# Hop-matrix building in a GNN kernel: 3, 2, 3, 2 sub-batches per turn in both passes, weighting on VectorE alone

## The chip, the cores and the metric

The kernel runs on one core of one Trainium2 chip. The metric is the device time of one execution in microseconds (us). Engines are named as the profile names them: PE is TensorE, PEld its weight loads, DVE is VectorE, ACT is ScalarE, POOL is GpSimd, SP is SyncE.

## The reference

Four graph layers run over the same 6,250 nodes (64 features) and 206,250 edges, which are sorted by destination. Each layer is `x = x + layer(relu(layernorm(x)))`:

```python
x = x + L0(h)   # h[src] @ W_msg + b, summed by dst; plus h @ W_self + b; rows divided by their norm
x = x + L1(h)   # h[src] @ W[type of the edge], summed by dst
x = x + L2(h)   # three hops of emb = segment_sum(w_e * emb[src], dst); mean of emb_0 .. emb_3
x = x + L3(h)   # an edge network's weight times h[src] @ W_src, summed by dst; plus h @ W_tgt
```

The three hops of L2 multiply by the same sparse matrix B (destination by source, with the edge weights as values).

## The kernel before

**Order of the work.** After a preparation of about 185 us, the kernel runs message pass 0 (layer L0), a projection that writes the relation table, message pass 1 (layer L1), the three hops (layer L2), and the edge pass (layer L3).

**A message pass.** The edges are cut into 1,664 steps (13 columns of 128) of 128 edges for one block of 128 nodes; 1,612 of them hold tiles of edges. Eight steps make a group (`G = 8`), four groups a turn (`R = 4`), so a pass has 208 groups in 52 turns (`ITER`). For each group:

- ACT copies eight index columns into `idx` (L739). The copy for group g + 3 waits for the products of group g.
- POOL starts eight indirect gathers of 128 rows (L540), which wait for that copy. Only 202 groups have gathers (`GQ`), 1,616 in a pass.
- DVE builds the one-hot tile `S` of the next group (L1312).
- PE multiplies `S` by the gathered rows (L977), into `ps[6]` and `ps[7]`.
- DVE adds the eight results into the accumulators (`accumulate`, L1326).

**Building B beside it.** B is needed only by the hops, and is built during the two message passes, as 62 chunks (`NCH`) of 16 sub-batches (`SUBS`), 992 in all. A sub-batch is `matrix_part`: DVE compares a column with an iota to make `ohp` in PSUM (L1366) and `Rc` (L1367), and multiplies `ohp` by the edge weights to make `Lw` (L1369). PE multiplies the two in 8 products (L959) and adds one to `bmm`, ACT copies the result to `stg` (L716) and adds one to `bev`, and SP writes each quarter of a chunk to `B_d` (L463). The buffers have two halves, so sub-batch u of DVE waits until the product of sub-batch u - 2 is done. Once per chunk the next chunk's records are loaded by SP (L447) and turned into columns by DVE, PE and ACT (L1331 to L1348, L944, L950, L707).

**How the sub-batches are spread.** `PER_TURN = (3, 2)`: every group of pass 0 builds three sub-batches, every group of pass 1 two, until the 62 chunks are done, which is after 46 of its 52 turns. Pass 0 builds 39 chunks (624 sub-batches), pass 1 23 (368). In pass 0 the second of the three sub-batches of a group is weighted by ACT (`by_scalar`, `weight_part`): DVE makes only `Rc` (L1363) and `ohp` (L1364) and ACT scales the eight slices one by one (L725). PE takes it by another semaphore, `lhs_a`.

**The loops.** `message_turns` unrolls whole bodies, because the half of a buffer and the place in a chunk must be constants: 8 turns in pass 0, 4 in pass 1 (`BODY`). In pass 0 turns 0 to 7 are written out, a loop runs over five bodies (turns 8 to 47), and turns 48 to 51 are written out; so the loop's branch is taken back four times.

Of the kernel before, what the change touches and what calls it, by code (L numbers as in the profile page):

```python
# [7 lines left out]
I32 = mybir.dt.int32  # L8
I16 = mybir.dt.int16
BF16 = mybir.dt.bfloat16  # L10
ALU = mybir.AluOpType
# [3 lines left out]
P = 128  # L15
# [6 lines left out]
def gnn_kernel(nc, x, src, dst, edge_attr, etype, eweight, msg_wt, msg_b, self_wt, self_b, lin, rel_w,  # L22
# [36 lines left out]
    SUBS = P // G  # L59
    PER_TURN = (3, 2)  # L60
    BODY = (8, 4)
    BUILT0 = ITER * R * PER_TURN[0] // SUBS
    FIRST = (0, BUILT0)
    CHUNKS = (BUILT0, NCH - BUILT0)
    BUILD_ITERS = tuple(k * SUBS // (R * t) for k, t in zip(CHUNKS, PER_TURN))
    assert all(i * R * t == k * SUBS and i <= ITER for i, k, t in zip(BUILD_ITERS, CHUNKS, PER_TURN)) and NCH <= KP
    assert all(b * R * t % (2 * SUBS) == 0 for b, t in zip(BODY, PER_TURN)) and min(BUILD_ITERS) > max(BODY)
    QS = SUBS // R
# [7 lines left out]
    PER_SLOT = [len(range(r, GQ, R)) for r in range(R)]  # L76
    assert NODE_BLOCKS - 1 <= (RS - 3) * G and GQ % (RS * R) >= R and GQ * G <= STEPS and (ITER - 3) * R + R - 1 < GQ - 3 + R

    with ExitStack() as ctx:
# [45 lines left out]
        def part(words):  # L125
# [39 lines left out]
        t0R = sb("t0R", [1, KP], I32)  # L165
        c128 = sb("c128", [P, NCH])
        ends = sb("ends", [P, 2])
        dcolAll = sb("dcolAll", [P, NCH])
        dvI = sb("dvI", [P, NCH], I32)
        dvH = sb("dvH", [P, NCH], I32)  # L170
        stepVi = sb("stepVi", [P, NCH], I32)
        stepV = sb("stepV", [P, NCH])
        start2 = sb("start2", [P, NC])
# [72 lines left out]
            mlp_Tc mlp_mm mlp_c web_in rec_out start_out start_in base_mm tcol_ok stair_f stair_T stair_e  # L246
            lhs_a types_in weights_in flat_ok flat_T flat_mv tiles_ok stair_done dve stair_d x_in ln_var ln_std ln_ok hs_ok hT_ps ht_ok proj_ps
            half_ps half_mv proj_mv nrm_in nrm_out idx_ok pc_ok rec2_out beg_oh beg_ps off_in off_ps tile_in tile_ps iota_ok
# [62 lines left out]
        def message_turns(n, eng, body):  # L311

            size, turn = BODY[n], PER_TURN[n]
            per_body = size * R * turn // SUBS

            def parts(b, k):
                at = [[(k * R + r) * turn + t for t in range(turn)] for r in range(R)]
                return [[(b * per_body + (FIRST[n] + o // SUBS), o % SUBS, (FIRST[n] + o // SUBS) % 2) for o in row] for row in at]

            def whole(b, count):  # L320
                for k in range(count):
                    body(b * size + k, parts(b, k))

            whole(0, size)
            with eng.Fori(1, BUILD_ITERS[n] // size) as b:
                whole(b, size)
            whole(BUILD_ITERS[n] // size, BUILD_ITERS[n] % size)
            if BUILD_ITERS[n] < ITER:
                none = [[] for r in range(R)]
                with eng.Fori(BUILD_ITERS[n], ITER - 3) as i:  # L330
                    body(i, none)
                for i in range(ITER - 3, ITER):
                    body(i, none)

        def next_chunk(row, pos):

            for c, at, h in row:
                if at == pos and not (isinstance(c, int) and c == NCH - 1):
                    return c + 1, 1 - h
            return None  # L340

        def by_scalar(n, t):

            return n == 0 and t == 1

        def weighted(n, g, t):

            if by_scalar(n, t):
                return s_["lhs_a"], g + 1
            if n == 0:  # L350
                return s_["lhs_ok"], g * 2 + (1 + (t > 1))
            return s_["lhs_ok"], g * PER_TURN[1] + (NG * 2 + t + 1)

# [153 lines left out]
        def _(pool):  # L507
# [9 lines left out]
            pool.iota(tile_i[:], [[P, NC]], base=0, channel_multiplier=1).then_inc(s_["pool_const"], 1)  # L517
            pool.iota(stepVi[:], [[P, NCH]], base=0, channel_multiplier=1).then_inc(s_["pool_const"], 1)

# [57 lines left out]
        def _(act):  # L577
# [139 lines left out]

            def weight_part(c, h, j):

                u = c * SUBS + j  # L720
                ohp = ps[2 + 3 * (j % 2)][:].rearrange("p (s k) -> p s k", s=G)
                act.wait_ge(s_["ohp_ok"], u + 1)
                for k in range(G):
                    at = 2 * P + j * G + k
                    ins = act.activation(Lw[:, j % 2, k, :], ohp[:, k, :], ACT.Copy, scale=cols[:, h, at:at + 1])  # L725
                ins.then_inc(s_["lhs_a"], 1)

            def message_pass(n, table):

                for r in range(R - 1):  # L730
                    act.wait_ge(s_["mm_ok"], n * NG + R)
                    act.copy(idx[:, r, :], table[:, r * G:(r + 1) * G]).then_inc(s_["idx_ok"], 1)

                def groups(i, parts):
                    for r in range(R):
                        if not (isinstance(i, int) and i * R + r + R - 1 >= GQ):
                            slot = (r + R - 1) % R
                            act.wait_ge(s_["mm_ok"], i * R + (n * NG + R + r + 1))
                            act.copy(idx[:, slot, :], table[:, bass.ds((i * R + (R - 1 + r)) * G, G)]).then_inc(s_["idx_ok"], 1)  # L739
                        for t, (c, pos, h) in enumerate(parts[r]):  # L740
                            if by_scalar(n, t + 1):
                                later = parts[r][t + 1]
                                weight_part(later[0], later[2], later[1])
                            matrix_part(c, pos)
                        ahead = next_chunk(parts[r], 9)
                        if ahead:
                            columns_of(*ahead)

                message_turns(n, act, groups)
# [98 lines left out]
        def _(pe):  # L848
# [103 lines left out]

            def matrix_part(n, g, t, c, j):

                pe.wait_ge(*weighted(n, g, t))
                wait(pe, s_["bev"], c * SUBS + (j - 1))
                for t in range(G):
                    a, i2 = t % 2, t // 2
                    ins = pe.matmul(ps[3 + j % 2][a * KP:(a + 1) * KP, i2 * KC:(i2 + 1) * KC], Lw[:, j % 2, t, :], Rc[:, j % 2, t, :],  # L959
                                    start=True, stop=True)  # L960
                ins.then_inc(s_["bmm"], 1)
# [3 lines left out]
            def segment(n):  # L965

                def groups(i, parts):
                    for r in range(R):
# [10 lines left out]
                        ins.then_inc(s_["mm_ok"], 1)  # L979
                        for t, (c, pos, h) in enumerate(parts[r]):  # L980
                            matrix_part(n, i * R + r, t, c, pos)
                        ahead = next_chunk(parts[r], 5)
# [134 lines left out]
        def _(dve):  # L1117
# [231 lines left out]

            def matrix_part(n, t, c, h, j):  # L1350
# [11 lines left out]
                if by_scalar(n, t):  # L1362
                    dve.tensor_tensor(Rc[:, j % 2, :, :], column(1, KC), iota_view(0, KC), ALU.is_equal)  # L1363
                    dve.tensor_tensor(ohp, column(0, KP), iota_view(0, KP), ALU.is_equal).then_inc(s_["ohp_ok"], 1)  # L1364
                    return
                dve.tensor_tensor(ohp, column(0, KP), iota_view(0, KP), ALU.is_equal).then_inc(s_["ohp_ok"], 1)  # L1366
                dve.tensor_tensor(Rc[:, j % 2, :, :], column(1, KC), iota_view(0, KC), ALU.is_equal)  # L1367
                dve.wait_ge(s_["ohp_ok"], u + 1)
                dve.tensor_tensor(Lw[:, j % 2, :, :], ohp, column(2, KP), ALU.mult).then_inc(s_["lhs_ok"], 1)  # L1369

            def message_pass(n, acc):
# [5 lines left out]
                def groups(i, parts):  # L1377
                    for r in range(R):
                        g = i * R + r
                        if not (isinstance(g, int) and g == NG - 1):  # L1380
                            one_hot(n, g + 1, (r + 1) % 2)
                        for t, (c, pos, h) in enumerate(parts[r]):
                            matrix_part(n, t, c, h, pos)
                        ahead = next_chunk(parts[r], 3)
# [40 lines left out]
            dve.sem_inc(s_["emb_ok"], 1)  # L1425
            chain(dve.tensor_scalar(dvI[:], dcolAll[:], float(PAD_DST), None, ALU.min))
            dve.tensor_scalar(dvH[:], dvI[:], 7, None, ALU.logical_shift_right)
# [129 lines left out]
```

## Time and profile before

| | |
|---|---|
| time, median of 3 runs | 8172.84 us (8172.44 to 8179.2) |
| profiled execution, its own time | 8187.84 us |
| span of the profiled execution | 8185.5 us |
| PE, DVE, ACT, POOL busy | 69%, 57%, 23%, 59% of the span |
| first gather of pass 0, first gather of pass 1 | 185.91 us, 2445.26 us |
| mean granted TensorE clock | 0.682 |

The span is the time from the first to the last instruction of one profiled execution, and it lies 2.3 us below that execution's own time. That execution was 15 us, or 0.18%, above the median. Busy shares are means over stages that are limited by different things, so they don't say what bounds a stage.

### The profile page before, as it was taken

The page shows a single profiled execution, that of the slowest core. Times are in us where ns is not written, and L with a number is a line of the kernel's source. Part 1 is how long each engine was busy: PE and PEld are TensorE (multiplying, and loading weights), DVE is VectorE, ACT ScalarE, POOL GpSimd, SP SyncE. Part 2 cuts the span into 40 slices and gives each one's busy share as a digit, 9 for nine tenths or more (in the row PEclk, how much of TensorE's full clock was granted, in tenths as well). Part 3 has the DMA queues.
Part 4 walks back from the last instruction along what each step waited for, and adds up shares of the span by engine and source line. Part 5 has one row for each costly group of instructions (what it writes and reads, how often), then busy time and mean ns, then how long its engine had stood idle before and what let it go on. Part 6 is the DMA issues. An engine that isn't in the chain of part 4 may idle for free.

```text
span 8185.5 us, 140527 instructions
## 1 busy us (share of the span) xinstructions
PE 5623.4 (69%) x42670; PEld 4173.2 (51%) x42671; DVE 4634.9 (57%) x10227; ACT 1864.4 (23%) x5982; POOL 4830.8 (59%) x5107
## 2 busy tenths in 40 slices
PE   3777666667755665566654777778768777877776
PEld 2666666666635555555554222222245555555555
DVE  5888888888856677777763000000045555555555
ACT  2333333333341111111110000000033333333333
POOL 1777777777707777777776111111137777777776
PEclk6666666666675656665665899999966666666666
DMA  6555555555644444444441999999933333333332
GB/s 192 90 92 92 92 89 92 88 93 88 92 163 69 71 69 71 73 72 69 71 73 39 400 426 405 426 406 426 426 101 81 83 81 82 82 81 83 81 82 68
DMA packets 795088, 1178.07 MB, mean 144 GB/s; under 512 B 617420, under 2 KB 645485, under 8 KB 766911
## 3 DMA queue, kind: packets, MB, share of 16 engines
q1 hardware_dynamic: 624379, 931.36, 37.7%
q0 software_dynamic: 164496, 230.86, 14.9%
q10 hardware_dynamic: 5684, 9.22, 0.4%
q8 instruction: 281, 4.60, 0.3%
q14 instruction: 248, 2.03, 0.1%
HBM read 919.30 MB, written 258.34 MB: 144 GB/s over the span
## 4 chain that ended last, share of the span: by engine, by line
POOL 31%; issue 19%; DMA 19%; PE 16%; DVE 12%; ACT 2%; DVEq 2%; SPq 0%; POOLq 0%; ACTq 0%
POOL arena L572 15%; POOL arena L540 15%; DMA arena<-B_d 13%; PE ps L1030 4%; PE ps L959 4%; PE ps L977 4%; DMA arena<-tab,idx 3%; DVE pair L1326 2%; DVE arena L1369 2%; DVE arena L1367 2%; DMA arena<-rec_d 2%; DVE ps L1366 2%; ACT arena L725 1%; DVEq L1318 1%; DVE arena L1363 1%
## 5 line engine op out<-in xcount | busy, mean ns | idle before, releaser
L540 POOL DMA_INDIRECT arena<-tab,idx x3232 | 3050.2, 944 | 1246.4 <-issue 1161.4
L572 POOL DMA_INDIRECT arena<-tab,idx x1664 | 1591.5, 956 | 647.1 <-issue 640.4
L977 PE MATMUL ps<-arena 128*128 x6656 | 1262.4, 369 | 897.4 <-DMA arena<-tab,idx 799.2
L959 PE MATMUL ps<-arena 128*64 128x98 f32 x15872 | 1322.3, 344 | 623.7 <-ACT arena L725 321.6
L977 PEld LDWEIGHTS ps<-arena 128*128 128x128 f32 x6656 | 1204.4, 280 | 969.1 <-issue 967.8
L959 PEld LDWEIGHTS ps<-arena 128*64 128x64 f32 x15872 | 1133.1, 203 | 754.9 <-issue 545.4
L1030 PE MATMUL ps<-arena,ev 128*64 128x512 f32 (+1 forms) x4836 | 1103.5, 602 | 363.3 <-DMA arena<-B_d 275.0
L1030 PEld LDWEIGHTS ps<-arena,ev 128*64 128x64 f32 x4836 | 391.4, 143 | 1075.1 <-issue 736.4
L563 POOL DMA_INDIRECT ev<-emb_d,dvI x186 | 175.1, 942 | 1268.2 <-PE ps L1030 1027.6
L1312 DVE TENSOR_TENSOR arena<-relT,ps 128x1024 f32<-128x1024 f32 x624 | 758.5, 1216 | 117.5 <-issue 114.7
L1441 DVE COPY pair<-ps 128x512 f32<-128x512 f32 x9 | 5.7, 684 | 1426.7 <-PE ps L1030 1426.7
L1367 DVE TENSOR_TENSOR arena<-arena,ps 128x784 f32<-128x784 f32 x784 | 754.2, 962 | 0.0
L1057 PE MATMUL ps<-ident,arena 128*64 128x128 f32 x3328 | 384.2, 406 | 451.3 <-DMA arena<-tab,idx 451.3
L716 ACT COPY arena<-ps 128x392 f32<-128x392 f32 x992 | 491.6, 496 | 811.8 <-PE ps L959 794.6
L1057 PEld LDWEIGHTS ps<-ident,arena 128*64 128x64 f32 x3328 | 302.5, 208 | 710.1 <-DMA arena<-tab,idx 708.6
L1366 DVE TENSOR_TENSOR ps<-arena,ps 128x512 f32<-128x512 f32 x784 | 540.9, 690 | 137.1 <-PE ps L959 134.8
L1504 DVE TENSOR_TENSOR pair<-pair,ps 64x128 f32 x1664 | 475.0, 285 | 209.4 <-PE ps L1092 119.7
L1326 DVE TENSOR_TENSOR pair<-pair,ps 128x64 f32 x2496 | 514.1, 219 | 112.2 <-issue 103.1
L1326 DVE TENSOR_TENSOR X<-X,ps 128x64 f32 x832 | 183.1, 220 | 643.3 <-PE ps L977 608.6
L1369 DVE TENSOR_TENSOR arena<-ps,arena 128x512 f32<-128x512 f32 x784 | 534.2, 681 | 0.0
L1476 DVE TENSOR_TENSOR arena<-ps,arena 128x512 f32<-128x512 f32 x208 | 143.7, 691 | 668.2 <-ACT arena L821 668.2
L814 ACT COPY arena<-arena 128x192 bf16 x1664 | 440.4, 347 | 126.8 <-issue 126.8
(244 smaller groups left out, 4982.4 us busy)
## 6 DMA issues: line engine op xcount, KB each, us to landing
arena<-B_d SPq DMA_DIRECT2D x186, 3136.0 KB, 24.8
B_d<-arena SPq DMA_DIRECT2D x248, 784.0 KB
arena<-tab,idx POOLq DMA_INDIRECT x4896
arena<-rel_d SPq DMA_DIRECT2D x208, 256.0 KB, 3.4
tab<-arena SPq DMA_DIRECT2D x26, 1024.0 KB, 3.9
arena<-rec_d SPq DMA_DIRECT2D x63, 257.5 KB
attr_s<-arena SPq DMA_DIRECT2D x13, 512.0 KB, 3.2
arena<-attr_s SPq DMA_DIRECT2D x208, 32.0 KB
```

Source lines behind the costliest of these rows:

```text
L540: pool.indirect_dma_start(ring[:, at:at + D], None, table, bass.IndirectOffsetOnAxis(ap=idx[:, k % R, u:u + 1], axis=0)).then_inc(gather_o ...
L572: pool.indirect_dma_start(gat[:, r, k * 2 * D:(k + 1) * 2 * D], None, tab3, bass.IndirectOffsetOnAxis(ap=idx[:, r, k:k + 1], axis=0)).then ...
L716: act.copy(stg[:, r % 2, j * w:(j + 1) * w], ps[3 + j % 2][:, 0:w]).then_inc(s_["bev"], 1)
L959: ins = pe.matmul(ps[3 + j % 2][a * KP:(a + 1) * KP, i2 * KC:(i2 + 1) * KC], Lw[:, j % 2, t, :], Rc[:, j % 2, t, :], start=True, stop=True)
L977: ins = pe.matmul(ps[6 + r % 2][:, k * D:(k + 1) * D], S[:, r % 2, k, :], ring[:, bass.ds(at[k], D)], start=True, stop=True)
L1030: ins = pe.matmul(ps[k][h * D:(h + 1) * D, 0:n], ev[:, u % EVS, :], Bb[:, u % BUFS, c0:c0 + n], start=c == 0, stop=c == NCH - 1)
L1057: pe.matmul(ps[h][t * D:(t + 1) * D, q * P:(q + 1) * P], gv[:, r, k, D:2 * D], ident[:], start=False, stop=True, skip_group_check=True)
L1312: dve.tensor_tensor(S[:, h, :, :], steps_of(relT, g), iota_view(n, P), ALU.is_equal).then_inc(s_["S_ok"], 1)
L1326: dve.tensor_tensor(a, a, ps[6 + r % 2][:, k * D:(k + 1) * D], ALU.add).then_inc(s_["acc_ok"], 1)
L1366: dve.tensor_tensor(ohp, column(0, KP), iota_view(0, KP), ALU.is_equal).then_inc(s_["ohp_ok"], 1)
L1367: dve.tensor_tensor(Rc[:, j % 2, :, :], column(1, KC), iota_view(0, KC), ALU.is_equal)
L1369: dve.tensor_tensor(Lw[:, j % 2, :, :], ohp, column(2, KP), ALU.mult).then_inc(s_["lhs_ok"], 1)
```

## The change

`PER_TURN` now gives the sub-batches of the four groups of a turn, 3, 2, 3 and 2, in both passes. A body is 16 turns in both passes: 160 sub-batches, 10 whole chunks. A pass is one body written out, a loop over two more (its branch is taken back once), and four turns written out (`TAIL`). In the four last turns pass 0 builds two sub-batches per group (two chunks more) and pass 1 none. Pass 0 so builds 32 chunks (512 sub-batches) and pass 1 30 (480). All weighting is done by DVE: `by_scalar`, `weighted`, `weight_part` and the semaphore `lhs_a` are gone. The records of one chunk past the last are now prepared too (63 in place of 62), and four small tiles are one column wider.

```diff
-    PER_TURN = (3, 2)
-    BODY = (8, 4)
-    BUILT0 = ITER * R * PER_TURN[0] // SUBS
+    PER_TURN = (3, 2, 3, 2)
+    BODY = 16
+    PER_BODY = BODY * sum(PER_TURN) // SUBS
+    BODIES = ITER // BODY
+    TAIL = ITER - BODIES * BODY
+    TAIL_TURN = 2
+    BUILT0 = BODIES * PER_BODY + TAIL * R * TAIL_TURN // SUBS
...
         def message_turns(n, eng, body):
...
-            whole(0, size)
-            with eng.Fori(1, BUILD_ITERS[n] // size) as b:
-                whole(b, size)
-            whole(BUILD_ITERS[n] // size, BUILD_ITERS[n] % size)
-            if BUILD_ITERS[n] < ITER:
-                none = [[] for r in range(R)]
-                with eng.Fori(BUILD_ITERS[n], ITER - 3) as i:
-                    body(i, none)
-                for i in range(ITER - 3, ITER):
-                    body(i, none)
+            def whole(b):
+                for k in range(BODY):
+                    at = [k * sum(PER_TURN) + sum(PER_TURN[:r]) for r in range(R)]
+                    body(b * BODY + k, [[place(b * PER_BODY, at[r] + t) for t in range(PER_TURN[r])] for r in range(R)])
+
+            whole(0)
+            with eng.Fori(1, BODIES) as b:
+                whole(b)
+            for k in range(TAIL):
+                row = TAIL_TURN if n == 0 else 0
+                body(BODIES * BODY + k, [[place(BODIES * PER_BODY, (k * R + r) * row + t) for t in range(row)] for r in range(R)])
...
-            def weight_part(c, h, j):
-
-                u = c * SUBS + j
-                ohp = ps[2 + 3 * (j % 2)][:].rearrange("p (s k) -> p s k", s=G)
-                act.wait_ge(s_["ohp_ok"], u + 1)
-                for k in range(G):
-                    at = 2 * P + j * G + k
-                    ins = act.activation(Lw[:, j % 2, k, :], ohp[:, k, :], ACT.Copy, scale=cols[:, h, at:at + 1])
-                ins.then_inc(s_["lhs_a"], 1)
...
-                pe.wait_ge(*weighted(n, g, t))
+                pe.wait_ge(s_["lhs_ok"], c * SUBS + (j + 1))
...
                 wait(dve, s_["bmm"], u - 1)
-                if by_scalar(n, t):
-                    dve.tensor_tensor(Rc[:, j % 2, :, :], column(1, KC), iota_view(0, KC), ALU.is_equal)
-                    dve.tensor_tensor(ohp, column(0, KP), iota_view(0, KP), ALU.is_equal).then_inc(s_["ohp_ok"], 1)
-                    return
                 dve.tensor_tensor(ohp, column(0, KP), iota_view(0, KP), ALU.is_equal).then_inc(s_["ohp_ok"], 1)
```

## Rows read from the trace of the kernel before

**Rows 1.** Busy time by stretch: both passes with tails, the projection, hops, edge pass

```profile
core 0: us, PE busy (x) PEld busy (x) DVE busy (x) ACT busy (x) POOL busy (x), PEclk, DMA share, GB/s
185.00:2245.00 2060.00, 1423.63 (x13150) 1283.41 (x13152) 1748.00 (x3621) 675.64 (x2437) 1524.23 (x1615) 0.64 0.57 90
2245.00:2326.00 81.00, 61.83 (x544) 56.20 (x542) 67.88 (x150) 26.11 (x90) 0.94 (x1) 0.58 0.41 65
...
2445.00:4462.00 2017.00, 1166.09 (x9324) 1083.16 (x9324) 1348.74 (x3039) 230.68 (x589) 1524.48 (x1616) 0.60 0.42 67
4462.00:4493.00 31.00, 24.15 (x112) 23.97 (x112) 15.97 (x62) 0.00 (x0) 0.57 (x1) 0.50 0.10 3
```

**Rows 2.** The gathers of pass 0: durations, first and last start, their engine's idle time

```profile
L540 POOL DMA_INDIRECT arena<-tab,idx x1616: 938/944/1032, 185.9 to 2245.3; - x180
...
  issue: 479.9, 1562
  ACT idx L739: 55.3, 53
```

**Rows 3.** The same for the gathers of pass 1

```profile
L540 POOL DMA_INDIRECT arena<-tab,idx x1616: 940/944/1068, 2445.3 to 4461.6; - x180
...
  issue: 681.5, 1584
  ACT idx L739: 9.8, 32
```

**Rows 4.** Timeline of POOL in pass 0: a gather that follows at once, the longest waits

```profile
1178.70 0.94 POOL L540 DMA_INDIRECT arena<-tab,idx  x1 [0.30 <-issue]
...
859.11 0.94 POOL L540 DMA_INDIRECT arena<-tab,idx  x1 [4.34 <-ACT idx L739]
1188.35 0.94 POOL L540 DMA_INDIRECT arena<-tab,idx  x1 [8.70 <-ACT idx L739]
1518.08 0.94 POOL L540 DMA_INDIRECT arena<-tab,idx  x1 [7.42 <-ACT idx L739]
1849.36 0.94 POOL L540 DMA_INDIRECT arena<-tab,idx  x1 [6.94 <-ACT idx L739]
```

**Rows 5.** Timeline of DVE and PE ahead of the wait at 1188 us

```profile
1177.00 1.22 DVE L1312 TENSOR_TENSOR arena<-relT,ps 128x1024 f32<-128x1024 f32 x1 [3.28 <-issue]
1179.03 0.68 PE L977 MATMUL ps<-arena 128*128 x2 [4.52 <-DVE arena L1312]
1183.95 3.25 PE L977 MATMUL ps<-arena 128*128 x14 [4.24 <-issue]
```

**Rows 6.** DVE by line, pass 0 with its tail: busy, mean ns, idle before

```profile
L1326 DVE TENSOR_TENSOR pair<-pair,ps 128x64 f32 x1664 | 331.3, 219 | 107.8 <-issue 103.1 <-DVE pair L1326 3.1
L1366 DVE TENSOR_TENSOR ps<-arena,ps 128x512 f32<-128x512 f32 x416 | 287.9, 692 | 137.1 <-PE ps L959 134.8 <-issue 1.8
```

**Rows 7.** Timeline of DVE in pass 1: one group with two sub-batches, next one's start

```profile
2987.49 1.22 DVE L1312 TENSOR_TENSOR arena<-relT,ps 128x1024 f32<-128x1024 f32 x1
2988.63 0.69 DVE L1366 TENSOR_TENSOR ps<-arena,ps 128x512 f32<-128x512 f32 x1
...
2990.71 0.69 DVE L1366 TENSOR_TENSOR ps<-arena,ps 128x512 f32<-128x512 f32 x1
...
2994.32 1.22 DVE L1312 TENSOR_TENSOR arena<-relT,ps 128x1024 f32<-128x1024 f32 x1
```

**Rows 8.** Timeline of pass 0's tail: a sub-batch for ACT, the last sums, the next step

```profile
2271.26 0.96 DVE L1363 TENSOR_TENSOR arena<-arena,ps 128x784 f32<-128x784 f32 x1
...
2272.86 1.74 ACT L725 ACTIVATE arena<-ps,arena 128x64 f32<-128x64 f32 x8 [5.76 <-DVE ps L1364]
...
2325.13 1.44 DVE L1326 TENSOR_TENSOR pair<-pair,ps 128x64 f32 x8
...
2326.61 0.96 DVE L1408 TENSOR_TENSOR pair<-pair 128x768 f32<-128x768 f32 x1
```

**Rows 9.** Timeline of pass 1's tail: last gather, products and sums after it

```profile
4461.63 0.94 POOL L540 DMA_INDIRECT arena<-tab,idx  x1 [0.30 <-issue]
4466.71 24.15 PE L977 MATMUL ps<-arena 128*128 x112 [8.80 <-DMA arena<-tab,idx]
4470.52 0.22 DVE L1326 TENSOR_TENSOR X<-X,ps 128x64 f32 x1 [9.55 <-PE ps L977]
```

**Rows 10.** What PE waited for in pass 1: us in total, times, longest

```profile
PE ps L977 <- DMA arena<-tab,idx: 772.5, 131, 20.8
```

**Rows 11.** Timeline of PE in pass 0's tail: a sub-batch, a group's products

```profile
2271.39 1.58 PE L959 MATMUL ps<-arena 128*64 128x98 f32 x16 [2.76 <-DVE arena L1369]
...
2277.46 3.68 PE L977 MATMUL ps<-arena 128*128 x16
```

**Rows 12.** ACT by line: copies of products, weighting

```profile
L716 ACT COPY arena<-ps 128x392 f32<-128x392 f32 x992 | 491.6, 496 | 811.8 <-PE ps L959 794.6 <-issue 16.7
...
L725 ACT ACTIVATE arena<-ps,arena 128x64 f32<-128x64 f32 x1664 | 362.7, 329 | 409.1 <-DVE ps L1364 398.8 <-issue 9.1
```

More of the change, by code:

```diff
@@ L59, in gnn_kernel @@
     SUBS = P // G
-    PER_TURN = (3, 2)
-    BODY = (8, 4)
-    BUILT0 = ITER * R * PER_TURN[0] // SUBS
+    PER_TURN = (3, 2, 3, 2)
[5 more added lines that the diff above has]
+    BUILT0 = BODIES * PER_BODY + TAIL * R * TAIL_TURN // SUBS
     FIRST = (0, BUILT0)
     CHUNKS = (BUILT0, NCH - BUILT0)
-    BUILD_ITERS = tuple(k * SUBS // (R * t) for k, t in zip(CHUNKS, PER_TURN))
-    assert all(i * R * t == k * SUBS and i <= ITER for i, k, t in zip(BUILD_ITERS, CHUNKS, PER_TURN)) and NCH <= KP
-    assert all(b * R * t % (2 * SUBS) == 0 for b, t in zip(BODY, PER_TURN)) and min(BUILD_ITERS) > max(BODY)
+    assert BODY * sum(PER_TURN) == PER_BODY * SUBS and PER_BODY % 2 == 0 and TAIL * R * TAIL_TURN % SUBS == 0
+    assert BUILT0 % 2 == 0 and CHUNKS[1] == BODIES * PER_BODY and BODIES > 2 and TAIL >= 3 and NCH < KP
     QS = SUBS // R
@@ L76, in gnn_kernel @@
     PER_SLOT = [len(range(r, GQ, R)) for r in range(R)]
-    assert NODE_BLOCKS - 1 <= (RS - 3) * G and GQ % (RS * R) >= R and GQ * G <= STEPS and (ITER - 3) * R + R - 1 < GQ - 3 + R
+    assert NODE_BLOCKS - 1 <= (RS - 3) * G and GQ % (RS * R) >= R and GQ * G <= STEPS
     with ExitStack() as ctx:
@@ L165, in gnn_kernel @@
         t0R = sb("t0R", [1, KP], I32)
-        c128 = sb("c128", [P, NCH])
+        c128 = sb("c128", [P, NCH + 1])
         ends = sb("ends", [P, 2])
-        dcolAll = sb("dcolAll", [P, NCH])
+        dcolAll = sb("dcolAll", [P, NCH + 1])
         dvI = sb("dvI", [P, NCH], I32)
         dvH = sb("dvH", [P, NCH], I32)
-        stepVi = sb("stepVi", [P, NCH], I32)
-        stepV = sb("stepV", [P, NCH])
+        stepVi = sb("stepVi", [P, NCH + 1], I32)
+        stepV = sb("stepV", [P, NCH + 1])
         start2 = sb("start2", [P, NC])
@@ L246, in gnn_kernel @@
             mlp_Tc mlp_mm mlp_c web_in rec_out start_out start_in base_mm tcol_ok stair_f stair_T stair_e
-            lhs_a types_in weights_in flat_ok flat_T flat_mv tiles_ok stair_done dve stair_d x_in ln_var ln_std ln_ok hs_ok hT_ps ht_ok proj_ps
+            types_in weights_in flat_ok flat_T flat_mv tiles_ok stair_done dve stair_d x_in ln_var ln_std ln_ok hs_ok hT_ps ht_ok proj_ps
             half_ps half_mv proj_mv nrm_in nrm_out idx_ok pc_ok rec2_out beg_oh beg_ps off_in off_ps tile_in tile_ps iota_ok
@@ L311, in message_turns, with place @@
         def message_turns(n, eng, body):
[L313 to L322, printed above, removed]
-            whole(0, size)
-            with eng.Fori(1, BUILD_ITERS[n] // size) as b:
-                whole(b, size)
-            whole(BUILD_ITERS[n] // size, BUILD_ITERS[n] % size)
-            if BUILD_ITERS[n] < ITER:
-                none = [[] for r in range(R)]
-                with eng.Fori(BUILD_ITERS[n], ITER - 3) as i:
-                    body(i, none)
-                for i in range(ITER - 3, ITER):
-                    body(i, none)
+            def place(c0, o):
+                return c0 + (FIRST[n] + o // SUBS), o % SUBS, (FIRST[n] + o // SUBS) % 2
+            def whole(b):
[8 more added lines that the diff above has]
+                body(BODIES * BODY + k, [[place(BODIES * PER_BODY, (k * R + r) * row + t) for t in range(row)] for r in range(R)])
         def next_chunk(row, pos):
             for c, at, h in row:
-                if at == pos and not (isinstance(c, int) and c == NCH - 1):
+                if at == pos:
                     return c + 1, 1 - h
             return None
-        def by_scalar(n, t):
-            return n == 0 and t == 1
-        def weighted(n, g, t):
-            if by_scalar(n, t):
[L349 to L352, printed above, removed]
         def column_turns(eng, body):
@@ L517, in _ @@
             pool.iota(tile_i[:], [[P, NC]], base=0, channel_multiplier=1).then_inc(s_["pool_const"], 1)
-            pool.iota(stepVi[:], [[P, NCH]], base=0, channel_multiplier=1).then_inc(s_["pool_const"], 1)
+            pool.iota(stepVi[:], [[P, NCH + 1]], base=0, channel_multiplier=1).then_inc(s_["pool_const"], 1)
             pool.wait_ge(s_["rec_out"], 16 * 7)
@@ L739, in groups @@
                             act.copy(idx[:, slot, :], table[:, bass.ds((i * R + (R - 1 + r)) * G, G)]).then_inc(s_["idx_ok"], 1)
[L740 to L743, printed above, removed]
+                        for c, pos, h in parts[r]:
                             matrix_part(c, pos)
@@ L951, in record_columns, with matrix_part @@
                 ins.then_inc(s_["recT"], 1)
-            def matrix_part(n, g, t, c, j):
-                pe.wait_ge(*weighted(n, g, t))
+            def matrix_part(c, j):
+                pe.wait_ge(s_["lhs_ok"], c * SUBS + (j + 1))
                 wait(pe, s_["bev"], c * SUBS + (j - 1))
@@ L979, in groups @@
                         ins.then_inc(s_["mm_ok"], 1)
-                        for t, (c, pos, h) in enumerate(parts[r]):
-                            matrix_part(n, i * R + r, t, c, pos)
+                        for c, pos, h in parts[r]:
+                            matrix_part(c, pos)
                         ahead = next_chunk(parts[r], 5)
@@ L1348, in record_weights, with matrix_part @@
                 dve.tensor_tensor(d2, d2, w, ALU.mult).then_inc(s_["row_d"], 1)
-            def matrix_part(n, t, c, h, j):
+            def matrix_part(c, h, j):
                 def column(f, w):
@@ L1361, in matrix_part @@
                 wait(dve, s_["bmm"], u - 1)
-                if by_scalar(n, t):
-                    dve.tensor_tensor(Rc[:, j % 2, :, :], column(1, KC), iota_view(0, KC), ALU.is_equal)
-                    dve.tensor_tensor(ohp, column(0, KP), iota_view(0, KP), ALU.is_equal).then_inc(s_["ohp_ok"], 1)
-                    return
                 dve.tensor_tensor(ohp, column(0, KP), iota_view(0, KP), ALU.is_equal).then_inc(s_["ohp_ok"], 1)
@@ L1381, in groups @@
                             one_hot(n, g + 1, (r + 1) % 2)
-                        for t, (c, pos, h) in enumerate(parts[r]):
-                            matrix_part(n, t, c, h, pos)
+                        for c, pos, h in parts[r]:
+                            matrix_part(c, h, pos)
                         ahead = next_chunk(parts[r], 3)
@@ L1425, in _ @@
             dve.sem_inc(s_["emb_ok"], 1)
-            chain(dve.tensor_scalar(dvI[:], dcolAll[:], float(PAD_DST), None, ALU.min))
+            chain(dve.tensor_scalar(dvI[:], dcolAll[:, 0:NCH], float(PAD_DST), None, ALU.min))
             dve.tensor_scalar(dvH[:], dvI[:], 7, None, ALU.logical_shift_right)
```

## The prediction, made before the changed kernel ran

> **What bounds the kernel now.** I first cut the span into stretches [rows 1]. The change touches only pass 0 with its tail (185 to 2326 us) and pass 1 with its tail (2445 to 4493 us); the projection between them, the hops and the edge pass keep their instructions. No engine is full in either pass, so the busy shares do not name the bound. In pass 0 DVE is nearest to it (1748 of 2060 us), in pass 1 POOL is (1524 of 2017 us).
>
> Next I read the gathers. In both passes POOL issues 1616 of them, 944 ns each. In pass 1 the first starts at 2445.3 and the last at 4461.6: 2016.3 us, or 1.248 us from one to the next. That is 0.944 us of work and 0.30 us of issue, and almost nothing of it is waiting: the index copies cost 9.8 us in 32 waits [rows 3]. PE on the other hand waits 772.5 us for gathered rows [rows 10]. So pass 1 runs at POOL's pitch, 8 x 1.248 = 9.98 us per group, and everything else has room.
>
> In pass 0 the same 1616 gathers take 2245.3 - 185.9 = 2059.4 us, 43.1 us more [rows 2]. A gather that does not wait follows at the same pitch (0.94 + 0.30 us, [rows 4]), so the excess is waiting, and the trace has it: 55.3 us on the index copies [rows 2], less some us that are the normal gap of those gathers. The longest waits, 4.34, 8.70, 7.42 and 6.94 us, lie about 330 us apart, which is eight turns of some 41 us, the length of a loop body [rows 4]. Just ahead of such a wait DVE stands 3.28 us and PE 4.52 and again 4.24 us inside a group of products, with no work to wait for in the second case [rows 5]. I read this as the loop's branch being taken back. The index copy waits for PE's products, and POOL for the copy.
>
> But a hiccup of 9 us every 330 us costs time only where there is no reserve. The copy is made three groups ahead, and in pass 1 the branch back shows nowhere in POOL's waits. In pass 0 the reserve is used up by DVE. Its ledger over pass 0 and the tail: busy 1748.0 + 67.9 = 1815.9 us [rows 1], waiting 134.8 us for the product of two sub-batches ago, and 103.1 us of issue ahead of the sums [rows 6], together 2053.8 of 2141 us; the rest is in small waits around the records and the branches. DVE is the paced engine of pass 0, at 2053.8 / 208 = 9.87 us per group before those small waits, against POOL's 9.98 us. There is no slack to repay a hiccup.
>
> **The cost of a sub-batch.** On DVE a sub-batch starts 2990.71 - 2988.63 = 2.08 us after the one before [rows 7]. One that ACT weights omits L1369 and costs DVE about 1.48 us (L1363 starts at 2271.26, its second instruction ends before ACT's start at 2272.86, [rows 8]). ACT then takes 1.74 us for it, later than DVE would have been by about a microsecond, and DVE's third sub-batch waits for its predecessors' products: the 134.8 us.
>
> **Pass 0.** DVE's sub-batch work was 416 x 2.08 + 208 x 1.48 = 1173 us and becomes 512 x 2.08 = 1065 us: 108 us less. The waits on PE stay in one group of two at most: with three sub-batches by DVE, PE needs 3.68 + 1.58 us for the group's products and its first sub-batch [rows 11], and DVE comes to the third after 1.14 + 2 x 2.08 = 5.3 us, a draw. I take 30 us of the 134.8 as left; the ends are 0 and 134.8. The ledger becomes 2053.8 - 108 - 105 = 1841 us; with the 87 us of small waits left as they are, 1928 us, 9.27 us per group, and 9.77 if all of the 134.8 us stay. One more set of records in pass 1 doesn't change this. Both lie under 9.98 us, so DVE gives the bound to POOL and keeps a reserve. A group with three sub-batches takes 1.14 + 3 x 2.08 + 1.5 = 8.9 us, one with two 6.83 us (2994.32 - 2987.49, [rows 7]); even the long one is shorter than POOL's group, so the alternation alone builds up no delay. The branch is taken back once, not four times, and its 9 us are repaid within some ten groups. Gathers of pass 0: 2059.4 -> 2016.3 us, **-43.1 us**. Upper bound of what stays: one wait of 9 us.
>
> **Its tail.** From the last gather of pass 0 to the first step behind it 2326.6 - 2245.3 = 81.3 us pass [rows 2, 8], because the groups 202 to 207 have no gathers but full building, and because PE is behind. Pass 1 shows what a punctual PE does: its products start 5.1 us and its sums 8.9 us after the last gather's start [rows 9]. The sums take 1.5 us, and six groups follow with two sub-batches each: 6 x 6.83 = 41 us, and I add 3.6 us for the next records' instructions and gaps. 8.9 + 1.5 + 41 + 3.6 = 55.0 us, **-26.3 us**. Bounds: 51.4 us with no gaps, and 60 us with 8 us per group.
>
> **Pass 1.** It gains 112 sub-batches, 112 x 2.08 = 233 us of DVE work, on 1348.7 + 16.0 us busy [rows 1]: 1598 us of 2048, under 8 us per group. PE gets 112 x 1.58 = 177 us more on 1190 us [rows 1, 11], ACT 112 copies of 0.5 us [rows 12]. DVE and PE do this while they wait for gathers now [rows 10]. SP's queue carries seven more chunks of four quarter writes each; the core's DMA share should rise from 0.42 towards 0.5, and pass 0 shows gathers issued at the same pitch at 0.57 [rows 1]. The last turns still build nothing (four in place of six), so the tail of 31 us stays. Price 0; if the cover fails, it is what DVE or PE then lacks. Bounds 0 and +20 us (two late phases of a branch and a chunk edge).
>
> **The sum.** 43.1 + 26.3 + 0 = 69.4 us. Against the profiled execution's own 8187.84 us this gives 8118.4 us. That execution lies 15.0 us over the median of the runs, so the median should be 8172.84 - 69.4 = **8103.4 us**, 0.85% faster. Weighting by ACT saved DVE 0.6 us each on 208 sub-batches; given back, this is 125 us more of DVE in total, all under POOL's pitch.
>
> A rule beside this: the Trainium skill, "Runtime: NRT & Kernel Launch", section "Instruction fetch mechanics", says that a taken branch whose target lies outside the loaded pages forces a fetch before the engine can go on. The trace agrees where the branch is taken back: 4.24 us without work on PE [rows 5]. By this rule alone only the branches matter, and the gain is that of the second case below.
>
> **The rivals.**
> *The branches were the whole loss, and the pace is not relieved.* Then of 4.34 + 8.70 + 7.42 + 6.94 = 27.4 us one wait of 6.9 us stays, the other 15.7 us of pass 0's excess stay, and the tail gains its 26.3 us: 46.8 us, 8126 us. For it: the waits sit at the bodies' ends. Against it: DVE's ledger is full between them too.
> *Pass 1 loses some of what pass 0 gains,* by later landings or by a branch in a busier consumer: +20 us there, and 10 us kept in pass 0: 8133 us. Against it: PE's 772.5 us of waiting are reserve.
> *Slower: three sub-batches weighted by DVE make DVE the pace in both passes.* Gathers and tails of both took 2140.7 + 2047.3 = 4188 us. With 85 us for both tails' fixed part, the break-even is (4188 - 85) / 404 = 10.15 us per group, a group mean 0.9 us above my 9.27. At 10.3 us the kernel would take 8231 us. It decides from 10.15 us up, and speaks for it only that a single group of pass 0 may hold a wait on PE that I put at nearly nothing.
> *Nothing is gained in the tail,* because what follows waits for the last chunk's write or another queue: 43.1 us alone, 8130 us. Against it: the next step is DVE's own, straight behind its sums [rows 8].
>
> **How the numbers follow.** My forecast has 0.76; the branches alone 0.07; the loss in pass 1 0.08; nothing in the tail 0.04; slower 0.03; the last 0.02 is no change in all. A measurement of this kernel can tell about 0.2%, 16 us. Faster by more: 0.95, within: 0.02, slower: 0.03. The time of the likeliest case is 8103 us. Below it only the tail's bound (3.6 us) and the runs' spread of some 6 us lie: 8092. Above it are the tail's 5 us, a wait of 9 us in pass 0, and the three middle cases: 8136.
>
> **What would show it.** The gathers of both passes span about 2016 us, with waits on index copies near 10 us each; about 55 us lie between pass 0's last gather and the first step behind its sums; DVE is busy some 125 us more, ACT some 363 us less [rows 12]; groups with three sub-batches take DVE about 8.9 us; pass 1's tail stays at 31 us. I am wrong if POOL still waits tens of us for copies, if either pass's gathers span over 2030 us, or if the stretches behind pass 1 change.

## The result, and the profile after

The changed kernel takes 8115.48 us, the median of 4 runs (8112.67 to 8117.69), against 8175.84 us for the kernel before, the median of 4 runs (8172.44 to 8179.2). The ratio is 0.9931, 95% interval [0.9919, 0.9943]: 0.7% faster, 60.4 us. 8103 us had been forecast, in a range of 8092 to 8136 us.

The profiled execution took 8112.67 us with a span of 8110.5 us, 75.0 us less than the profiled span of before. The same stretches as in [rows 1], with the same columns, of the changed kernel:

```profile
185.00:2200.00 2015.00, 1378.76 (x11455) 1255.38 (x11456) 1629.53 (x3483) 298.17 (x726) 1523.11 (x1615) 0.60 0.42 81
...
2373.00:4389.00 2016.00, 1332.54 (x11196) 1211.34 (x11196) 1582.54 (x3423) 289.79 (x709) 1523.95 (x1615) 0.62 0.41 79
```

The two passes are now alike, with about 1600 us of DVE work each. The gathers of pass 0 and then of pass 1, as in [rows 2, 3] (L525 was L540):

```profile
L525 POOL DMA_INDIRECT arena<-tab,idx x1616: 940/944/972, 184.3 to 2200.4; - x180
...
  ACT idx L714: 9.4, 31
```

```profile
L525 POOL DMA_INDIRECT arena<-tab,idx x1616: 940/944/1008, 2373.2 to 4389.3; - x180
```

Both passes' gathers span 2016.1 us. The waits on index copies are 31 in each pass, 9.4 us in all, which is the normal gap of 0.30 us each. After the first gather, POOL's timeline of pass 0 has no longer gap.

The stretches of the profiled executions, each from the starts of the first and last gathers of a pass and of the first step behind its sums (in pass 0 L1408, now L1376; in pass 1 L1421, now L1389). "Again" is a second profile of the kernel before, which is explained below:

| us | before | again | after | before to after |
|---|---|---|---|---|
| up to the first gather | 185.9 | 183.8 | 184.3 | -1.6 |
| pass 0, gathers | 2059.4 | 2035.8 | 2016.1 | -43.3 |
| pass 0, tail | 81.3 | 77.4 | 52.2 | -29.1 |
| to pass 1's first gather | 118.7 | 119.4 | 120.6 | +2.0 |
| pass 1, gathers | 2016.3 | 2016.5 | 2016.1 | -0.2 |
| pass 1, tail | 30.9 | 30.8 | 30.8 | -0.1 |
| the rest | 3692.9 | 3690.6 | 3690.4 | -2.5 |

The first step behind the tail of pass 0, as in [rows 8]:

```profile
2252.53 0.96 DVE L1376 TENSOR_TENSOR pair<-pair 128x768 f32<-128x768 f32 x1
```

The branch still stalls the engines. This is where the loop of pass 0 is taken back, as in [rows 5]:

```profile
1474.23 1.22 DVE L1284 TENSOR_TENSOR arena<-relT,ps 128x1024 f32<-128x1024 f32 x1 [2.98 <-issue]
...
1476.71 1.75 PE L949 MATMUL ps<-arena 128*128 x7 [4.53 <-issue]
...
1480.66 2.18 PE L949 MATMUL ps<-arena 128*128 x9 [2.20 <-issue]
```

DVE stands 2.98 us, PE 4.53 and again 2.20 us inside one group's products. POOL doesn't wait for it, because the copy that depends on these products is still 9.4 us ahead of the gather that needs it.

DVE's waits for PE in pass 0 with its tail, as in [rows 6] (L1334 was L1366):

```profile
L1334 DVE TENSOR_TENSOR ps<-arena,ps 128x512 f32<-128x512 f32 x512 | 352.6, 689 | 211.1 <-PE ps L931 210.8
```

DVE waits more for PE than before, 210.8 us against 134.8 us, and still the pass is shorter.

**The reserve.** One quantity is used in all that follows. It is the time from the end of the index copy that group k's products release to the start of the first gather of group k + 3. It was worked out for all 199 copies of a pass from the timelines of ACT and POOL. Where it is about 0.8 us or less, POOL has waited for the copy.

| reserve in pass 0, us | first copy | groups 100 to 127 | first copies after the branch at group 128 | groups 140 to 190 |
|---|---|---|---|---|
| before | 14.7 | 0.8 to 6.7 | 0.8, 3.5, 2.8 | 0.3 to 9.3 |
| after | 14.8 | 10.3 to 16.2 | 9.4, 10.4, 15.2 | 9.3 to 16.3 |

### The profile page after: what moved, and what is told of

It is laid out like the page before. It is cut to its first block, busy times and chain, and to the rows that moved or that the text cites. A ratio compares the mean times of both kernels' runs of the same rounds, so it can differ in the third digit from the quotient of the medians.

```text
span 8110.5 us, 137608 instructions
## 1 busy us (share of the span) xinstructions
PE 5719.3 (71%) x42680; PEld 4250.9 (52%) x42681; DVE 4728.7 (58%) x10441; ACT 1528.0 (19%) x4319; POOL 4829.1 (60%) x5107
## 4 chain that ended last, share of the span: by engine, by line
POOL 42%; issue 20%; DMA 18%; PE 13%; DVE 5%; DVEq 1%; ACT 1%; POOLq 0%; ACTq 0%; SPq 0%
POOL arena L525 26%; POOL arena L557 16%; DMA arena<-B_d 13%; PE ps L1002 4%; PE ps L949 4%; DMA arena<-tab,idx 4%; PE ps L931 1%; DVE ps L1334 1%; DVE arena L1337 1%; PE ps L899 1%; DMA tab<-arena 1%; DVE pair L1298 1%; DVE arena L1335 1%; DMA emb_d<-pair 1%; PE ps L1029 0%
## 5 line engine op out<-in xcount | busy, mean ns | idle before, releaser
L525 POOL DMA_INDIRECT arena<-tab,idx x3232 | 3049.7, 944 | 1176.2 <-issue 1137.3
L949 PE MATMUL ps<-arena 128*128 x6656 | 1344.5, 387 | 912.1 <-DMA arena<-tab,idx 843.8
L949 PEld LDWEIGHTS ps<-arena 128*128 128x128 f32 x6656 | 1281.1, 296 | 989.4 <-issue 987.7
L931 PE MATMUL ps<-arena 128*64 128x98 f32 x15872 | 1340.2, 346 | 432.5 <-DVE arena L1337 422.9
L1335 DVE TENSOR_TENSOR arena<-arena,ps 128x784 f32<-128x784 f32 x992 | 956.9, 965 | 0.0
L1334 DVE TENSOR_TENSOR ps<-arena,ps 128x512 f32<-128x512 f32 x992 | 683.1, 689 | 424.1 <-PE ps L931 423.8
L1337 DVE TENSOR_TENSOR arena<-ps,arena 128x512 f32<-128x512 f32 x992 | 678.8, 684 | 0.0
L1444 DVE TENSOR_TENSOR arena<-ps,arena 128x512 f32<-128x512 f32 x208 | 143.9, 692 | 672.7 <-ACT arena L793 672.7
L1025 PE MATMUL ps<-arena,Web 17*128 17x512 f32 x416 | 345.9, 923 | 29.1 <-DMA arena<-attr_s 29.1
```

Of the source, the lines that this page charges most:

```text
L525: pool.indirect_dma_start(ring[:, at:at + D], None, table, bass.IndirectOffsetOnAxis(ap=idx[:, k % R, u:u + 1], axis=0)).then_inc(gather_o ...
L949: ins = pe.matmul(ps[6 + r % 2][:, k * D:(k + 1) * D], S[:, r % 2, k, :], ring[:, bass.ds(at[k], D)], start=True, stop=True)
```

## The experiments

All ratios are against runs of the kernel before on the same chip. The line numbers of the rows are those of each kernel.

**A body of 16 turns, nothing else.**

```diff
-    BODY = (8, 4)
+    BODY = (16, 4)
```

> The kernel before with a loop body of 16 turns in place of 8 in pass 0, nothing else: the loop's branch is taken back once, not four times, in pass 0. Theory A (VectorE paces pass 0, the branches add to it): VectorE still makes the three sub-batches per group at about 10.1 us per group, so pass 0's gathers still span over 2035 us; the time falls by 10 to 27 us, to some 8150 to 8165. Theory B (the branches were the whole loss of pass 0, and VectorE's load does not matter): the gathers span about 2025 us, with one wait of 7 to 9 us, and the time falls by 35 us or more, to 8140 or less. No change at all would mean that the stalls at the branch don't come from the branch.

Measured: 8143.59 us (8142.09 to 8151.23, 5 runs), ratio 0.9964, 95% interval [0.9950, 0.9978]. The gathers of pass 0:

```profile
L540 POOL DMA_INDIRECT arena<-tab,idx x1616: 938/944/1033, 182.7 to 2203.9; - x180
```

They span 2021.2 us, 4.9 us over pass 1's. (The edit also takes eight more turns out of the loop, turns 8 to 15.) This number is that of theory B, the branches alone, and not that of A. The time lies between the two forecasts: it fell by 29.6 us, where A had 10 to 27 us and B 35 us or more. The tail stays at 80.6 us. The reserve starts at 14.8 us and is still there at group 63. It is 8.4 us at group 127, with no branch taken back until then, falls to 1.1 us at the one branch at group 128, and stays between 0.5 and 9.9 us to the end. So with this load the groups in the loop win back little of what a branch took, and lose some 5 us in 64 groups without one.

**VectorE weights all, 3 and 2 as before.**

```diff
         def by_scalar(n, t):
-            return n == 0 and t == 1
+            return False
...
             if n == 0:
-                return s_["lhs_ok"], g * 2 + (1 + (t > 1))
-            return s_["lhs_ok"], g * PER_TURN[1] + (NG * 2 + t + 1)
+                return s_["lhs_ok"], g * 3 + (t + 1)
+            return s_["lhs_ok"], g * PER_TURN[1] + (NG * 3 + t + 1)
```

> The kernel before with ScalarE's weighting given to VectorE, 3 and 2 sub-batches per group as before. Theory A (VectorE's ledger): VectorE gets 208 x 0.6 = 125 us more in pass 0 and loses some 105 of its 135 us of waits on the product of two sub-batches ago; pass 0 is 20 us longer, about 2161 us with its tail, and the time is about 8195 us. Rival C (the detour over ScalarE was what held pass 0 up): pass 0's gathers come back to POOL's pitch, 2016 us, and the time falls by some 30 to 45 us. Theory B (branches alone): no change, within 5 us.

Measured: 8221.19 us (8210.99 to 8230.36, 5 runs), ratio 1.0052 [1.0038, 1.0067]. Pass 0 is longer, and its waits more:

```profile
L540 POOL DMA_INDIRECT arena<-tab,idx x1616: 942/947/1066, 184.6 to 2277.7; - x180
...
  ACT idx L739: 81.6, 64
```

The gathers span 2093.1 us. Here the load itself exceeds POOL's pitch: the reserve is at 0.8 us by group 45, before the first branch (it is at group 64), and stays between 0.3 and 5.3 us. From 14.8 to 0.8 us in 45 groups is 0.31 us per group over POOL's 9.98 us: a group with three sub-batches weighted by VectorE takes 10.3 us in the mean here. The sign of theory A's expectation holds, but pass 0 with its tail is 37 us longer and the time 48 us, where it had about 20 us; rival C is refuted. In the old spread ScalarE's help was worth about 48 us.

**ScalarE weights one of three again, in the changed kernel.** The edit puts `weight_part` and `lhs_a` back, for the second sub-batch of the groups with three, in both passes:

```diff
+        def by_scalar(row, t):
+            return len(row) == 3 and t == 1
...
+                if scaled:
+                    dve.tensor_tensor(Rc[:, j % 2, :, :], column(1, KC), iota_view(0, KC), ALU.is_equal).then_inc(s_["lhs_ok"], 1)
+                    dve.tensor_tensor(ohp, column(0, KP), iota_view(0, KP), ALU.is_equal).then_inc(s_["ohp_ok"], 1)
+                    return
```

> The changed kernel, but in every group with three sub-batches the second one is weighted by ScalarE as before, in both passes. Theory A (only VectorE's mean load against POOL's pitch counts, and the spread is what lowered it): VectorE has 192 x 0.6 = 115 us less to do, but it was under the pitch already, so nothing moves: gathers of 2016 us in both passes, time within 4 us of the changed kernel, 8115 us. Rival C (the detour over ScalarE costs): POOL waits again, and the kernel is 10 to 40 us slower than the changed one.

Measured: 8118.08 us (8114.68 to 8125.10, 5 runs), ratio 0.9931 [0.9917, 0.9945], the changed kernel's own ratio. Both passes' gathers span 2016.5 and 2016.3 us. With ten sub-batches per turn, who weights makes no difference that these runs can tell.

**Pass 0's last sub-batches moved ahead of group 202.**

```diff
-    TAIL_TURN = 2
+    TAIL_ROWS = ((4, 3, 3, 3), (4, 3, 3, 3), (3, 3, 0, 0), (0, 0, 0, 0))
```

> The changed kernel with the 32 sub-batches of pass 0's four last turns moved ahead of group 202: rows of 4, 3, 3, 3; 4, 3, 3, 3; 3, 3, 0, 0; 0, 0, 0, 0. Theory A (the tail of pass 0 is VectorE's building in groups that have no gathers, and the reserve of three groups takes the dense rows): the tail falls from 52.2 us to between 31 and 36 us, the time by 16 to 21 us against the changed kernel, to 8095 to 8100 us. Rival D (the dense rows use up the reserve, ten groups of some 10.5 us against 9.98 us): POOL waits for index copies there, 5 to 10 us of the gain are lost. Rival E (the last chunk's write or the projection's start holds the end): the tail shortens, and the stretch to pass 1's first gather grows by as much; no gain.

Measured: 8102.33 us (8101.49 to 8115.11, 5 runs), ratio 0.9914 [0.9899, 0.9929]. The last gather of pass 0 starts at 2202.4 us and the step behind the sums here:

```profile
L1378 DVE TENSOR_TENSOR pair<-pair x2: 957/1892/2826, 2239.1 to 2250.9; 128x768 f32<-128x768 f32 x1, 128x2560 f32<-128x2560 f32 x1
```

The tail is 36.7 us, 15.5 us less than the changed kernel's, and the gathers stay at 2016.4 us; the reserve did not go under 9.3 us in the dense rows. The stretch to pass 1's first gather is 121.1 us, against 120.6 us. Theory A holds and D and E don't, though the tail is 0.7 us and the time 2 us above A's ranges. The 12 sub-batches that stood in the groups without gathers are 12 x 2.08 = 25 us of DVE, so not all of their time came back.

**The same, denser at the front.**

```diff
-    TAIL_ROWS = ((4, 3, 3, 3), (4, 3, 3, 3), (3, 3, 0, 0), (0, 0, 0, 0))
+    TAIL_ROWS = ((4, 4, 4, 3), (4, 3, 3, 3), (2, 2, 0, 0), (0, 0, 0, 0))
```

> The changed kernel with the 32 sub-batches of pass 0's last turns moved ahead of group 202, more of them at the front: rows of 4, 4, 4, 3; 4, 3, 3, 3; 2, 2, 0, 0; 0, 0, 0, 0. If the 36.7 us of the first such tail are 31 us of pass 1's kind and a lag of VectorE in the last dense groups, this one comes to 32 to 34 us, and the time to about 8098 us. If the dense rows empty the reserve (lowest was 9.3 us there), POOL waits and nothing is gained over 8102 us.

Measured: 8102.51 us (8101.59 to 8109.67, 5 runs), ratio 0.9917 [0.9903, 0.9930]. The tail is 38.7 us, no shorter, and the reserve fell to 5.1 us. POOL still did not wait. The expected 32 to 34 us were not reached. What the 6 and 8 us are by which these two tails exceed pass 1's was not followed.

**The two passes' loads exchanged.** Two sub-batches per group in pass 0, three in pass 1 with the second by ScalarE, four branches back in each. `by_scalar` and `weighted` are exchanged to match, and the four small tiles have the changed kernel's width:

```diff
-    PER_TURN = (3, 2)
-    BODY = (8, 4)
+    PER_TURN = (2, 3)
+    BODY = (8, 8)
```

> The kernel before with the two passes' loads exchanged: two sub-batches per group in pass 0 (all by VectorE), three in pass 1 (the second by ScalarE), and a loop body of 8 turns in both, so that each pass takes its branch back four times. Theory F (a branch costs nothing where the groups between two of them are shorter than POOL's and so refill the reserve of index copies; it costs its stall where they are not): pass 0 with the same four branches as before runs at POOL's pitch, 2016 to 2018 us, and its tail takes 52 us; pass 1 now shows the loss, 2045 to 2065 us. Time 8172 - 43 - 29 + 43 = about 8143 us. Theory B (branches at this spacing cost whatever the load is): both passes' gathers span 2040 us or more, and the time is not under 8165 us.

Measured: 8138.07 us (8122.76 to 8139.85, 5 runs), ratio 0.9952 [0.9939, 0.9966]. The gathers of pass 0 and then of pass 1:

```profile
L540 POOL DMA_INDIRECT arena<-tab,idx x1616: 940/944/1043, 183.2 to 2200.2; - x180
```

```profile
L540 POOL DMA_INDIRECT arena<-tab,idx x1616: 938/944/1067, 2370.1 to 4417.8; - x180
```

Pass 0 with the same four branches as before takes 2017.0 us, with a reserve that never goes under 9.2 us, and pass 1 takes 2047.7 us. Pass 0's tail is 51.7 us with two sub-batches per group. The loss went with the load. Theory F holds, B does not.

**Pass 0 without a loop.** All 52 turns written out, the old load and the old weighting:

```diff
-    BODY = (8, 4)
+    BODY = (52, 4)
...
             whole(0, size)
+            if n == 0:
+                return
```

> The kernel before with pass 0 written out whole, 52 turns without a loop, its load of three sub-batches per group and the weighting by ScalarE unchanged. Theory F: the pace of the groups alone is only some 0.08 us per group over POOL's 9.98 us (the reserve of the run with 16-turn bodies fell from 14 to 5 us in 124 groups), so without any branch the reserve of 14 us lasts for nearly the whole pass: gathers 2016 to 2020 us, tail about 80 us, time about 8140 us, 0 to 5 us under the run with 16-turn bodies. Theory A as predicted (VectorE has no slack between the branches either): waits of POOL spread over the pass, gathers over 2025 us.

Measured: 8137.99 us (8129.63 to 8149.86, 5 runs), ratio 0.9961 [0.9948, 0.9975]. The gathers of pass 0:

```profile
L541 POOL DMA_INDIRECT arena<-tab,idx x1616: 940/944/1062, 187.1 to 2203.9; - x180
```

2016.8 us: POOL's pitch, at three sub-batches per group. The reserve stays between 7.1 and 16.6 us over the whole pass, and the 0.08 us per group that were expected over POOL's pitch don't show. Theory A, with waits of POOL all over the pass and over 2025 us, is refuted. The tail is 75.1 us. DVE by line, pass 0 with its tail (L1313 was L1312, L1327 L1326, L1367 L1366):

```profile
L1327 DVE TENSOR_TENSOR pair<-pair,ps 128x64 f32 x1664 | 299.7, 220 | 98.9 <-issue 91.1 <-DVE pair L1327 5.8
L1367 DVE TENSOR_TENSOR ps<-arena,ps 128x512 f32<-128x512 f32 x416 | 288.0, 692 | 173.4 <-PE ps L960 172.4 <-issue 0.8
L1313 DVE TENSOR_TENSOR arena<-relT,ps 128x1024 f32<-128x1024 f32 x208 | 252.7, 1215 | 0.4 <-issue 0.4
```

DVE's stalls ahead of the one-hot tile are gone: 0.4 us, against 17.5 us in the kernel before. But this run took away more than branches. The same 1,664 sums keep DVE busy for 299.7 us, against 331.3 us [rows 6]. Inside a loop the eight sums of a group take 1.65 us, in written-out turns 1.44 us ([rows 8] has such a group), which is 0.2 us per group less work for DVE. A row from the loop, out of the run with 16-turn bodies:

```profile
1479.29 1.65 DVE L1326 TENSOR_TENSOR pair<-pair,ps 128x64 f32 x8
```

So the run shows that the load fits under POOL's pitch in written-out code. It doesn't show that it does so inside a loop, where the reserve of the run with 16-turn bodies fell from 13.7 us at group 64 to 8.4 us at group 127 without a branch.

**The kernel before once more.**

> The kernel before, unchanged, for a second profile of it. If its profiled time moves with the span of pass 0's gathers (which was 2059 us in an execution of 8187.8 us) and all other stretches stand, then the scatter of this kernel, 8160.9 to 8191.7 us in nine runs against 8112.7 to 8117.7 us in four of the changed kernel, is that of pass 0, which has no reserve. If the gathers again span 2059 us whatever the time is, the scatter lies elsewhere.

Measured: 8167.53 us (8156.54 to 8182.70, 10 runs), ratio 0.9997 [0.9987, 1.0006]. Its profiled execution took 8156.54 us:

```profile
L540 POOL DMA_INDIRECT arena<-tab,idx x1616: 938/944/1042, 183.8 to 2219.6; - x180
```

Between the two profiled executions of the same kernel, 31.3 us apart, pass 0 with its tail differs by 27.5 us (2140.7 and 2113.2 us, the sums from the table above), and all other stretches together by 3.7 us. As far as two profiles can tell, the scatter of the kernel before, 8156.5 to 8191.7 us over all runs, is that of pass 0.

## Why the prediction was right, and where not

**The range and the direction** held: pass 0's gathers came back to POOL's pitch (43.3 us, forecast 43.1), the tail fell to 52.2 us (forecast 55.0), pass 1's price was nothing, its tail stayed. The sum of 69.4 us stands against 75.0 us in the profiled spans.

**The likeliest time, 8103 us, was 12 us too low,** and not for one of the mechanisms. The excess of 43.1 us was read from one execution and subtracted from the median of others. That execution was 15.0 us above the median, and the second profile shows that such a difference lies in pass 0: there the same kernel has only 19.5 us of excess over POOL's pitch and a tail of 77.4 us. The term was right for the execution that it was read from, and too large for the median as far as these two profiles tell. The prediction carried the 15.0 us along as if they lay elsewhere.

**The step that failed is the ledger, by which DVE was the paced engine of pass 0.** It added DVE's waits to its busy time and found the pass full. But an engine that works in step with others always fills its pass, once its waits are counted as its own. The run without a loop shows it at the same sub-batches per group: there the wait on PE rises from 134.8 to 172.4 us, in a pass (with its tail) that is 48.8 us shorter. The changed kernel shows it too: the 30 us that I put are 210.8 us, seven times as much, and still POOL never waits. So the forecast of 2016.3 us for pass 0's gathers came true beside a term that was wrong by 180 us, because the true limit, POOL's pitch, doesn't depend on it.

**The conclusion drawn from the ledger holds in part.** It was that pass 0 has no slack to repay a stall. At three sub-batches per group, inside a loop, the reserve indeed comes back little or not at all. But the loss itself came with the branches: one in place of four takes 38.2 of 43.1 us in the profiled spans, or 14.6 of 19.5 us against the second profile. The rival that the branches were the whole loss of pass 0's gathers was nearly right about the kernel before. Its price was not: it left the 15.7 us outside the four long waits where they were, and the run with one branch shows that most of them also go with the branches. It is wrong where the load is lighter: there the same four branches cost nothing. The load decides whether a stall reaches the end.

The long group was mis-sized as well. I took 8.9 us for a group with three sub-batches, and concluded that even the long one is shorter than POOL's. With all groups of that kind the mean is 10.3 us, waits and records included. It is the mean over threes and twos that lies under 9.98 us.

A rule beside this: the Trainium skill, "Runtime: NRT & Kernel Launch", section "Instruction fetch mechanics", has a taken branch out of the loaded pages force a fetch before the engine goes on. The runs agree that the stalls are the branch's: without the loop they are gone (0.4 us against 17.5 us ahead of DVE's one-hot tile). They don't show that it is a fetch.

**What holds in its place.** POOL's 9.98 us per group is the pace of both passes. The index copies run three groups ahead, a reserve of about 15 us. In the passes with twelve sub-batches per turn, a branch back takes some 7 to 12 us of it, counting what POOL then waits. In the old pass 0 a group took about as long as POOL's eight gathers, so that little was paid back. In the first profile 7.3 us were left ahead of group 64, and the first branch used them up; in the second it was the second branch, at group 96, which found 8.0 us. From then on the copies are often just in time, and small waits follow between the branches too. The change does two things about this. One branch in place of four is nearly enough by itself, and a lighter load is enough by itself at eight sub-batches per turn; ten per turn with four branches was not run. The experiments:

| pass 0 or 1, gathers, us | four branches | one or none |
|---|---|---|
| twelve per turn, one in three by ScalarE | 2059.4, 2035.8; 2047.7 (pass 1) | 2021.2; 2016.8 |
| ten per turn | not run | 2016.1; 2016.1 |
| eight per turn | 2017.0 | not run |

Pass 1 of the kernel before belongs here too: at eight per turn and four turns in a body it takes its branch back nine times, DVE stands about 3 us at each, and its gathers span 2016.3 us. With the lighter load PE stands waiting for gathered rows anyway, 772.5 us in that pass [rows 10].

**Where the 60 us come from,** by the timed runs: the branches alone give 29.6 us (8173.15 to 8143.59) or, without a loop, 34.4 us (8172.37 to 8137.99). Both include the shorter sums of the turns that no longer lie in a loop. The rest, about 26 to 31 us, is for the most part the tail, which two sub-batches per group in place of three shorten from between 75 and 81 us to 52 us (51.7 us in the run with exchanged loads).

**All weighting by VectorE** costs nothing in the new spread and 48 us in the old one. I had priced it at nothing for the right reason, the room under POOL's pitch, though the room was smaller than I said: in the old spread the 125 us of work lengthened pass 0 by 37 us against the first profile and 64.5 us against the second.

**What would have shown me wrong** did not appear: no waits of tens of us, no pass over 2030 us, no change behind pass 1. ACT's busy time fell from 1864.4 to 1528.0 us, 336 us where 363 us were forecast; DVE's rose by 94 us, forecast 125 us. In the changed kernel the groups of three could not be timed by themselves as forecast, since most of them hold a wait.

**A better version.** The changed kernel with pass 0's last sub-batches moved ahead of the groups without gathers takes 8102.33 us. On the same chip the changed kernel's twin with ScalarE's weighting took 8118.08 us. The changed kernel itself was not run beside it; it took 8115.48 us in runs of its own. The ratios to the kernel before, 0.9914 and 0.9931, have intervals that overlap; the profiled tails differ by 15.5 us.

**Open:** why the two profiles of the kernel before lose so differently at the same branches was not settled. The core's DMA share in pass 0 was about 0.57 in one and 0.48 in the other, at the same traffic, and no run tests what that does. It can't be the whole of the loss: the run without a loop had a share of 0.49, like the second profile, and 19 us less in pass 0's gathers.

## What to carry to other kernels

Where one engine sets the pace and others run ahead of it by a few buffers, ask of a stall not how long it is but whether the reserve is full again before the next one; measure the reserve from the two timelines. Don't add an engine's waits to its busy time to call it full: take the load away or the stall away, one at a time. And a loss read from one profile may be subtracted only from that execution's time, above all in a stage that has no reserve: here nearly all of the scatter lay there. When a loop is written out to take a branch away, check what else in its body became shorter. Work beside a paced engine should not be placed where that engine is done: moving 12 sub-batches out of such groups took 15.5 us off the tail.

## What the runs showed of the hardware

Where a loop is taken back, the engines stood still: DVE for 2.9 to 3.4 us at every branch of the kernel before and the changed one, with bodies of 4, 8 or 16 unrolled turns; PE 4.5 us, and 2.2 to 4.2 us more a few products later, in the rows shown ([rows 5] and those of the changed kernel). In pass 1 of the run without a loop in pass 0, DVE stood 8.6 to 9.5 us at each of nine branches; why is open, and the gathers there span 2016.4 us all the same.

Eight sums of a group took DVE 1.65 us inside a loop and 1.44 us in written-out turns.

The pitch of the indirect gathers was 1.248 us (0.944 us and 0.30 us between two) in every pass that was not held up, with spans of 2016.1 to 2017.0 us. It was so at DMA shares of 0.41 and 0.42 with DVE busy for 67% to 81% of the pass, and in the pass without a loop, which has the old load, at a share of 0.49. The one exception is pass 1 of the run in which VectorE weights all: 2020.6 us, without a wait for a copy beyond the normal gap.
